# A graph network with a mixture of experts: where a projection's weight block is made, the group sizes of the third normalization, and the engine that writes its tiles

## The reference

```python
x = x + _L0_gnn_ref(_layernorm(x), edge_index, ...)   # mean over neighbours, matmul, relu, row norm
x = x + _L0_ffn_ref(_layernorm(x)[None], ...)[0]      # 8 experts, top 2 per token
x = x + _L1_gnn_ref(_layernorm(x), edge_index, ...)   # graph attention, 8 heads of 32
x = x + _L1_ffn_ref(_layernorm(x)[None], ...)[0]      # shared MLP and 4 experts, top 2
```

## Time and profile before

| | us |
|---|---|
| median of 3 runs | 3578.93 |
| lowest, highest | 3575.56, 3579.14 |
| the profiled execution: its own time | 3576.32 |
| its span, first to last instruction | 3574.6 |

### The profile page before, as it was taken

How to read it: one execution, slowest core, us unless ns; L and a number is a source line. 1 busy time by engine, 2 the same in 40 slices (tenths; PEclk the granted TensorE clock), 3 DMA queues, 4 the chain that set the end, 5 groups by cost and what they waited for, 6 DMA issues and landing times. The chain is left out here.

```text
span 3574.6 us, 54480 instructions
## 1 busy us (share of the span) xinstructions
PE 2776.7 (78%) x13194; PEld 2280.1 (64%) x13195; DVE 1849.9 (52%) x4502; ACT 1146.4 (32%) x4187; POOL 1719.6 (48%) x1811
## 2 busy tenths in 40 slices
PE   1477788888876699999999437777677776768999
PEld 0366666666664588888888325555555554557888
DVE  4324454454557211111111747888888888866664
ACT  3001010000001122222222235555555556534554
POOL 0777777777771123222222057777777777600000
PEclk9988888898887899999999768888888888888999
DMA  5333334333331222222221634433333334300000
GB/s 163 114 105 111 109 109 116 110 110 109 110 110 32 77 83 86 87 83 86 88 85 34 191 106 110 108 105 108 105 106 104 107 106 110 92 21 14 19 19 21
DMA packets 152340, 327.85 MB, mean 92 GB/s; under 512 B 38839, under 2 KB 90001, under 8 KB 148034
## 3 DMA queue, kind: packets, MB, share of 16 engines
q0 software_dynamic: 85824, 236.38, 23.5%
q1 hardware_dynamic: 53494, 76.64, 6.3%
q10 hardware_dynamic: 12844, 12.82, 1.1%
HBM read 286.42 MB, written 41.40 MB: 92 GB/s over the span
## 5 line engine op out<-in xcount | busy, mean ns | idle before, releaser
L684 POOL DMA_INDIRECT G<-g_rows,srcT x784 | 742.7, 947 | 392.6 <-issue 236.7
L684 POOL DMA_INDIRECT G<-h_rows,srcT x784 | 753.3, 961 | 238.8 <-issue 237.6
L849 PE MATMUL pS<-G,O 128*128 x2336 | 565.1, 406 | 169.4 <-issue 98.2
L1760 PE MATMUL pS<-G,O 128*128 x2336 | 627.2, 431 | 37.8 <-DVE O L1908 29.8
L849 PEld LDWEIGHTS pS<-G,O 128*128 128x128 f32 x2336 | 473.7, 205 | 257.3 <-issue 180.0
L1760 PEld LDWEIGHTS pS<-G,O 128*128 128x128 f32 x2336 | 485.0, 211 | 174.6 <-issue 62.9
L1825 ACT ACTIVATE G<-G 128x32 f32<-128x32 f32 x2352 | 503.2, 307 | 0.0
L1418 ACT ACTIVATE HE<-pH,b1s 128x256 f32<-128x256 f32 x432 | 204.4, 473 | 584.2 <-PE pH L1393 584.2
L1393 PE MATMUL pH<-XT,w1s 128*128 128x256 f32 x1728 | 384.2, 381 | 1.2 <-SPq L1364 1.2
L1403 PE MATMUL pY<-w2s,HE 128*128 128x256 f32 x1728 | 382.0, 380 | 0.0
L1325 POOL DMA_INDIRECT y_rows<-YE,yidx x108 | 109.3, 1012 | 527.8 <-DVE YE L1445 511.4
(11 more groups left out here) (292 smaller groups left out, 3512.4 us busy)
## 6 DMA issues: line engine op xcount, KB each, us to landing
w1s<-in_W_dram SPq DMA_DIRECT2D x16, 1024.0 KB, 4.9
w2s<-in_W_dram SPq DMA_DIRECT2D x16, 1024.0 KB, 7.8
G<-h_rows,srcT POOLq DMA_INDIRECT x784, 2.8
Y<-y_rows SPq DMA_DIRECT2D x49, 256.0 KB, 4.6
G<-g_rows,srcT POOLq DMA_INDIRECT x784, 2.8
g_rows<-OUT SPq DMA_DIRECT2D x49, 132.0 KB, 2.4
h_rows<-ACC SPq DMA_DIRECT2D x7, 896.0 KB, 4.0
out_dram<-X SPq DMA_DIRECT2D x48, 128.0 KB
```

The costliest lines, as they stand in the source:

```text
L684: pool.indirect_dma_start(out=G[:, c % (ring * Q), 0:width], out_offset=None, in_=rows, in_offset=bass.IndirectOffsetOnAxis(ap=srcT[:, c:c ...
L849: mm = nc.tensor.matmul(pS[k][:, 0:W], O[:, k, q, :], G[:, bass.ds((s % R0) * Q + q, 1), :].rearrange("p a d -> p (a d)"), start=(q == 0), ...
L1760: mm = nc.tensor.matmul(pS[:, bass.ds((w % BANKS) * BANK, NR)], O[:, k, q, :], G[:, bass.ds((s % R) * Q + q, 1), 0:NR].rearrange("p a d -> ...
```

## The change

The weight block moves into the expert stage. ACT issues the four transfers at its start, ahead of its loop; POOL writes the index tiles after its first two fetches; DVE makes A after the first pair; PE multiplies after its loop, into a PSUM bank (`pL[0]`) that routing has left; DVE copies the product after its own loop. In the third-normalization stage the groups become 3, 4, five times 7, 4 and 3 tiles (`PG`, with `PF` the first tile of each); SP loads 14 tiles without a break; DVE's `normal` now ends with a column `shift` (minus mean times rstd); and ACT writes `IN` (`normal_in`), two tiles ahead of the tile that it copies out. Where only moved code is taken away, the diff is cut.

```diff
@@ -1271,8 +1271,24 @@
             clear_spent()
 
             HALVES = z.TOK // P
+            HW = HC + 1
+            GR = HEADS * HW
+            sb, ps, sem = make(route)
+            Wrow = sb("Wrow", [P, KD, GR + HEADS])
+            WpT = sb("WpT", [P, KD, D])
+            att = sb("att", [P, KD, 2])
+            head_of = sb("head_of", [P, KD], I32)
+            head_f = sb("head_f", [P, KD])
+            hh = sb("hh", [P, HEADS])
+            A = sb("A8", [P, KD, 2, HEADS])
             with ExitStack() as ctx:
                 sb, ps, sem = make(ctx)
+                pW = pL[0]
+                s_w = sem("s_w8")
+                s_iota = sem("s_iota8")
+                s_A = sem("s_A8")
+                s_wmm = sem("s_wmm8")
+                s_dve = sem("s_dve6")
                 w1s = sb("w1s", [P, 2, KD, z.HID])
                 w2s = sb("w2s", [P, 2, KH, D])
                 b1s = sb("b1s", [P, 2, KH])
@@ -1330,6 +1346,9 @@
                         n = pairs_used(pool)
                         fetch(0, 0)
                         fetch(1, 1)
+                        nc.gpsimd.iota(head_of[:], pattern=[[P, KD]], base=0, channel_multiplier=1).then_inc(s_iota, 1)
+                        nc.gpsimd.iota(hh[:], pattern=[[1, HEADS]], base=0, channel_multiplier=0,
+                                       allow_small_or_imprecise_dtypes=True).then_inc(s_iota, 1)
                         with pool.Fori(0, n) as i:
                             for k in range(2):
                                 fetch(i * 2 + k + 2, k)
@@ -1403,10 +1422,23 @@
                                         mm = nc.tensor.matmul(pY[h][:, 0:D], HE[:, b, h * P:(h + 1) * P], w2s[:, k, b, :],
                                                               start=(b == 0), stop=(b == KH - 1))
                                 mm.then_inc(s_ymm, 1)
+                        pe.wait_ge(s_A, 1)
+                        for m in range(KD):
+                            for j in range(KD):
+                                mm = nc.tensor.matmul(pW[:, m * 2 * HEADS:(m + 1) * 2 * HEADS],
+                                                      WpT[:, j, m * P:(m + 1) * P],
+                                                      A[:, j].rearrange("p c h -> p (c h)"), start=(j == 0), stop=(j == KD - 1))
+                        mm.then_inc(s_wmm, 1)
 
                     @block.scalar
                     def _(act):
                         act.sem_inc(s_ycp, 3)
+                        act.dma_start(WpT[:], a["WpT"].rearrange("(k p) n -> p k n", p=P)).then_inc(s_w, 16)
+                        act.dma_start(att[:], a["att"].rearrange("(k p) n -> p k n", p=P)).then_inc(s_w, 16)
+                        for m in range(KD):
+                            act.dma_start(Wrow[:, m, 0:GR].rearrange("p (h c) -> p h c", c=HW)[:, :, 0:HC],
+                                          a["Wp"][m * P:(m + 1) * P, :].rearrange("p (h c) -> p h c", c=HC))\
+                                .then_inc(s_w, 16)
                         n = pairs_used(act)
                         with act.Fori(0, n) as i:
                             for k in range(2):
@@ -1449,39 +1481,46 @@
@@ -1449,39 +1481,46 @@
                         token_index(1, 1)
                         copy_turned(0, 0)
                         turn(0, True)
+                        loc = Local(dve, s_dve)
+                        dve.wait_ge(s_iota, 2)
+                        loc.link(nc.vector.tensor_single_scalar(head_of[:], head_of[:], HC.bit_length() - 1,
+                                                                op=ALU.arith_shift_right))
+                        loc.link(nc.vector.tensor_copy(head_f[:], head_of[:]))
+                        dve.wait_ge(s_w, 16 * (2 + KD))
+                        for m in range(KD):
+                            for c in range(2):
+                                loc.tick(nc.vector.tensor_scalar(A[:, m, c], hh[:], head_f[:, m:m + 1],
+                                                                 att[:, m, c:c + 1], ALU.is_equal, ALU.mult))
+                        loc.settle()
+                        dve.sem_inc(s_A, 1)
                         with dve.Fori(1, n) as i:
                             turn(i, False)
-
-
-            HW = HC + 1
-            GR = HEADS * HW
+                        dve.wait_ge(s_wmm, 1)
+                        pw = pW[:, 0:KD * 2 * HEADS].rearrange("p (k c h) -> p k c h", k=KD, c=2)
+                        wr = Wrow[:, :, 0:GR].rearrange("p k (h c) -> p k h c", c=HW)
+                        loc.tick(nc.vector.tensor_copy(wr[:, :, :, HC], pw[:, :, 0, :]))
+                        loc.link(nc.vector.tensor_copy(Wrow[:, :, GR:GR + HEADS], pw[:, :, 1, :]))
+
+
             with ExitStack() as ctx:
                 sb, ps, sem = make(ctx)
                 SLOTS, INS = 14, 8
+                PG = (3, 4) + (UNROLL,) * 5 + (4, 3)
+                PF = [sum(PG[:g]) for g in range(len(PG) + 1)]
+                assert PF[-1] == NT
...
-                A = sb("A8", [P, KD, 2, HEADS])
+                shift = sb("shift8", [P, NT])
...
-                pW = ps("pW8", [P, 512])
...
-                s_wcp = sem("s_wcp8")
+                s_norm = sem("s_norm8")
...
@@ -1504,15 +1543,7 @@
-                        for t in range(UNROLL):
-                            load(t)
-                        sp.dma_start(WpT[:], a["WpT"].rearrange("(k p) n -> p k n", p=P)).then_inc(s_w, 16)
...
-                        for t in range(UNROLL, SLOTS):
+                        for t in range(SLOTS):
                             load(t)
...
-                    @block.gpsimd
-                    def _(pool):
-                        nc.gpsimd.iota(head_of[:], pattern=[[P, KD]], base=0, channel_multiplier=1).then_inc(s_iota, 1)
...
-                        def sums(t0):
+                        def sums(g):
+                            t0, t1 = PF[g], PF[g + 1]
                             add0(t0)
-                            for t in range(t0 + 1, t0 + UNROLL):
...
+                        def variance(g):
+                            dve.wait_ge(s_stat, PF[g + 1])
+                            ln_group(loc, PF[g], PF[g + 1])
                             dve.sem_inc(s_var, 1)
 
-                        def normal(t0):
-                            dve.wait_ge(s_root, t0 // UNROLL + 1)
-                            ln_group_rstd(loc, t0, t0 + UNROLL)
-                            for t in range(t0, t0 + UNROLL):
-                                if t >= INS:
-                                    dve.wait_ge(s_turned, t - INS + 1)
-                                ln_apply(IN[:, t % INS], X[:, t, :], slice(t, t + 1)).then_inc(s_in, 1)
+                        def normal(g):
+                            dve.wait_ge(s_root, g + 1)
+                            ln_group_rstd(loc, PF[g], PF[g + 1])
+                            v = slice(PF[g], PF[g + 1])
+                            loc.link(nc.vector.scalar_tensor_tensor(out=shift[:, v], in0=mean[:, v], scalar=-1.0,
+                                                                    in1=rstd[:, v], op0=ALU.mult, op1=ALU.mult))
+                            dve.sem_inc(s_norm, 1)
 
                         sums(0)
                         variance(0)
-                        sums(UNROLL)
-                        variance(UNROLL)
-                        normal(0)
-                        dve.wait_ge(s_iota, 2)
-
...
-                        dve.sem_inc(s_A, 1)
-                        dve.wait_ge(s_wmm, 1)
-                        pw = pW[:, 0:KD * 2 * HEADS].rearrange("p (k c h) -> p k c h", k=KD, c=2)
-                        wr = Wrow[:, :, 0:GR].rearrange("p k (h c) -> p k h c", c=HW)
-                        nc.vector.tensor_copy(wr[:, :, :, HC], pw[:, :, 0, :]).then_inc(s_wcp, 1)
-                        nc.vector.tensor_copy(Wrow[:, :, GR:GR + HEADS], pw[:, :, 1, :]).then_inc(s_wcp, 1)
-                        for t0 in range(2 * UNROLL, NT, UNROLL):
-                            sums(t0)
-                            variance(t0)
-                            normal(t0 - UNROLL)
-                        normal(NT - UNROLL)
+                        for g in range(1, len(PG)):
+                            sums(g)
+                            variance(g)
+                            normal(g - 1)
+                        normal(len(PG) - 1)
@@ -1615,14 +1621,25 @@
-                        def root(t0):
-                            act.wait_ge(s_var, t0 // UNROLL + 1)
-                            ln_group_root(t0, t0 + UNROLL).then_inc(s_root, 1)
+                        def root(g):
+                            act.wait_ge(s_var, g + 1)
+                            ln_group_root(PF[g], PF[g + 1]).then_inc(s_root, 1)
+
+                        def normal_in(t):
+                            act.wait_ge(s_norm, [t < e for e in PF[1:]].index(True) + 1)
+                            if t >= INS:
```

(60 more changed lines are left out.)

19 lines of the change are left out of this document (removed).

## The result

The changed kernel takes 3570.36 us (median of 20 runs, 3566.25 to 3572.99). The kernel before, run on the same chip beside it, takes 3581.34 (20 runs, 3574.0 to 3587.74). The ratio is 0.9969, with a 95% interval of 0.9963 to 0.9975: a gain of 11.0 us. The forecast was 3565; the range, 3560 to 3573, holds the result.

A forecast was written before the change was run, and what follows sets the result against it. VectorE was taken to set the third-normalization stage's pace, TensorE's end the next stage's start. Terms -13.1 + 0.5 = -12.6 against 3576.3 gave 3563.7; with the runs' median 2.6 higher, the forecast was put midway at 3565, range 3560 to 3573.

The forecast's parts named there:

- What bounds the kernel: Third-normalization stage: VectorE sets the pace after the weight block; any shift of TensorE's end at 2081.83 reaches kernel end whole.
- What VectorE sheds: Third-normalization stage: seven tiles of IN (2.35 us) leave VectorE, a shift of 0.24 joins; a group of 7 costs 9.60.
- The tail: Stage's end: from tile 28 at 2042.7, TensorE projects 22 tiles at 1.137, ending near 2068.7; gain 13.1 us.
- the prediction's own signs: Trace rows named beforehand as showing it right (projection tiles at 1.14) or wrong (ScalarE never idle while TensorE waits).
- the first rival: Third-normalization stage: ScalarE becomes the pace, 2.4 us lost at 1.25 per tile, 8.9 at 1.54; 3567 to 3574; chance 0.17.
- the last rival: Third-normalization stage: ScalarE and TensorE take turns, 1.65 per tile, slower than before, 3580 to 3585 us; chance 0.04.
- The four transfers: Expert stage's start: ScalarE's loads for the weight block mostly fall into empty DMA time; price taken as 0.5 us.
- the interleaving of the rival: Expert stage's start: none of the 0.52 MB falls into empty DMA time, weights come 2.4 us later; 3567; chance 0.06.
- The covered edits: Expert stage: ScalarE's issues, index tiles, making A, matmuls and copies hide behind other work; uncovered 5, 0.3, 1.3 and 2.2 us.
- The clock: Rival, third-normalization stage: TensorE's clock falls between groups at tile 28, costing 1.5 to 3 us; 3567; chance 0.06.
- Loads and stores: Rival, middle of third-normalization stage: bunched transfers stall it 4 to 8 us, giving 3569 to 3573; chance 0.03.
- ScalarE instead of VectorE: Third-normalization stage: by the skill's rule alone, 49 tiles at 0.51 for 0.34 would cost 8.3 us more engine time.

The follow-up runs named there:

- the order of the tail: Changed kernel, but from tile 28 on ScalarE copies the next tile's transpose first, then writes IN three tiles ahead, then copies the product out; ratio to before 0.9960.
- the groups alone: Kernel before with only the groups of 3, 4, five times 7, 4 and 3 tiles; ratio to before 0.9989, stage 104.65 us.
- ScalarE's writes alone: Kernel before with only ScalarE writing the normalized tiles, two ahead; groups of 7 and weight block stay; ratio to before 0.9977, stage 99.29 us.
- Three tiles ahead: Changed kernel with ScalarE writing the normalized tile three ahead instead of two, throughout the stage; ratio to before 0.9974, stage 98.38 us.

## Why the prediction was right, and where it was off

**What bounds the kernel.** Right. VectorE's full middle, the weight block ahead of TensorE's first tile and TensorE's end as the start of the next stage are what the change acted on, and the gain in TensorE's end arrives whole.

**What VectorE sheds.** Right in size, and the last digit by luck. Its groups of 7 come every 9.68 us (9.60 worked out). Shift and reciprocal with their links take 0.56 per group where 0.48 stood. From VectorE's first addition to the write of tile 28 there are 2043.20 - 1983.62 = 59.58 us, where the working had 59.6, but two errors cancel in that: the wait for the second load, which is part of it, was 0.24 and not 0.90, and the work itself took 0.6 more. Against the issue of the stage's first load tile 28 came 0.75 us late (63.26 for 62.5). The two loads make only 0.14 of that (3.68 + 0.24 against 2.88 + 0.90); the rest is VectorE's work.

**The tail: the step that was off.** "ScalarE's sum 1.13 per tile, just under TensorE's 1.137" was right as a sum, since with the order of the tail ScalarE kept up with TensorE's own pace. But the step took the sum of a queue for its pace, and said that the new instruction costs nothing more in steady state since it stands two tiles ahead. In the order of the change it stands between the copy-out of one tile and the copy to HT of the next, on the path from product to product, and the pair of tiles takes 2.49 us. So the 22 tiles took 27.2 us (2044.13 to 2071.32) where 25.0 were forecast. With the 0.75 by which tile 28 was late that makes up, to 0.1, the 2.9 us by which TensorE's end missed its gain: 10.26 (101.64 us after the stage's first load before, 91.38 after) against 13.1.

Of the prediction's own signs, projection tiles at 1.14 and a last product 25 us after the wait did not come, and ScalarE without idle time while TensorE waits for IN, a sign of being wrong, nearly did: 17.23 of 18.00, with TensorE's weight load standing 0.23 us for IN at 2058.89. In pace this is the first rival at its mild end, 1.25 per tile and 2.4 us lost; in mechanism it is not, as that rival had ScalarE's time itself run out. The order of the queue stands in the last rival (ScalarE and TensorE take turns), but with the write running only after a tile's product, at 1.65 per tile; here it runs beside the next product (2058.24, in the product from 2057.91 to 2059.09).

**The four transfers.** Right in kind, and 0.28 us where 0.5 was taken (14.44 against 14.16; 0.11 to 0.63 in the other runs with that code). By the interleaving of the rival it would have been 2.4.

**The covered edits.** Right. The matmuls for W times A run at 1964.68 (0.96 us) and the two copies at 1965.68 and 1965.77, while POOL's last scatters start at 1966.53 and 1967.85; from the first product to the next stage's first load the trace shows 0.09 us less than before.

**The clock.** Right. The granted clock is 0.98 and 1.00 in the two stretches above; TensorE's wait for tile 28 was 0.66 us. The hole was worked out at 1.6; it was smaller because the seven tiles before it took 9.0 us (9.68 less 0.66) and not 7.96, so the slow loop itself helped to keep the clock. With the groups alone, where the hole was 3.43 us, the clock did fall.

**Loads and stores.** The stall that this rival named does occur, but small: 1.57 and 0.67 us in two runs of the same stage, and 1.74 in three waits with ScalarE's writes alone. Three tiles ahead made it grow.

**ScalarE instead of VectorE.** The Trainium skill ("ScalarE: Activation LUTs", section "Rules for kernel authors") sends additions and products to VectorE. The price per tile agrees in direction (0.49 us from start to start on ScalarE, 2.35 / 7 = 0.34 on VectorE), but the path decides: the dearer engine had room, and alone this part gave 6.11 us.

**The time.** The sum was -12.6, the stage and the transfers gave -10.0, and the medians -11.0. The forecast of 3565 stood on 3577.6 for the kernel before (3565 + 12.6), which ran at 3581.34 in these runs: that is 3.7 of the 5.4 us between 3565 and 3570.36, and the smaller gain is 1.6. The result lies outside the forecast's own range (3560 to 3568) and in the first rival's (3567 to 3574). Much of that is the level of the kernel before in these runs, so the time by itself does not tell the two apart; the rows of the tail do.

## What to carry to other kernels

When an instruction is added to an in-order queue, its time is only half of the question. Trace the loop from one result back to the same result a few tiles on, through every queue that it passes, and put the instruction that nobody waits for soon behind the one that somebody waits for now: here that order, with the write three tiles ahead, was worth 0.11 us per tile, and three tiles ahead in the old order nothing. When a producer works in groups, the release of a group can move ahead of the next group's sums, but then the short answer that it needs from another engine must be placed where that engine has already come by.

## What was not expected

- ScalarE ran at 17.84 of 18.00 us busy without slowing TensorE, with four instructions of 0.63, 0.41, 0.40 and 0.19 us (1.63 in sum) in 1.13 us: from start to start they take 0.49, 0.27, 0.27 and 0.05, so that successive ones overlap by a third of their length.
- The first load of Y brought VectorE's first addition 2.65 to 3.68 us after its issue over the twelve traces. In the changed kernel a shorter wait for the second load made up for most of the difference (2.88 + 0.90 before, 3.68 + 0.24 after).
